# Expert tiles of the last sequence moved ahead of its attention output, and twelve instead of eight ahead of the tail

## The reference, cut to what matters

```python
def _L1_ffn_ref(x, Wg, W1, b1, W2, b2):
    logits = xt @ Wg.T
    topk_logits, topk_idx = jax.lax.top_k(logits, TOP_K)      # 2 of 8 experts for each row
    w = jax.nn.softmax(topk_logits, axis=-1)
    h = jax.nn.gelu(jnp.einsum('th,ehi->tei', xt, W1) + b1)   # 128 -> 512
    o = jnp.einsum('tei,eih->teh', h, W2) + b2                # 512 -> 128
    y = jnp.einsum('te,teh->th', gates, o)
...
x = x + linear_and_window_attention(xn) + gated_ffn(xn)
xn = _layernorm(x)
x = x + causal_attention(xn) + _L1_ffn_ref(xn)
```

## Time and profile before

| | us |
|---|---|
| median of 3 runs | 1281.19 |
| lowest, highest | 1279.73, 1285.44 |
| profiled execution | 1279.02 |
| its span, first to last instruction | 1277.3 |
| dense stage of the last sequence, from the last window score to `prefix` | 51.8 |
| maxima stage of the tail, with 29 tiles | 79.5 |
| from there to the end, with 41 tiles | 121.3 |

### The profile page before, as it was taken

One profiled execution on the slowest core, in us unless ns is written; L12 is line 12 of the kernel. 1 busy time (PEld: TensorE's weight loads), 2 busy tenths in 40 slices (PEclk: granted clock), 3 DMA queues, 4 the chain that ended last, 5 costly groups with the idle time before them and its releaser, 6 DMA issues.

```text
span 1277.3 us, 26679 instructions
## 1 busy us (share of the span) xinstructions
PE 1152.3 (90%) x9122; PEld 743.5 (58%) x9122; DVE 865.0 (68%) x3433; ACT 743.6 (58%) x1580; POOL 649.1 (51%) x846
## 2 busy tenths in 40 slices
PE   5988999998999899989998999899989867988997
PEld 2445754574457545754575457544754556874896
DVE  4066588658865886588558865886588656874563
ACT  2356357735773577457745774567546624557675
POOL 4475254535444544454444544454445435685577
PEclk9999999999999999999999999999999978999999
DMA  7601620162015301540154015401571016541233
GB/s 237 156 3 47 186 72 14 55 184 75 13 56 160 99 14 52 139 121 15 43 150 120 15 40 151 119 17 40 152 224 44 2 26 147 83 68 27 44 55 40
DMA packets 123961, 105.53 MB, mean 83 GB/s; under 512 B 15242, under 2 KB 118578, under 8 KB 123826
## 3 DMA queue, kind: packets, MB, share of 16 engines
q1 hardware_dynamic: 102162, 85.89, 24.6%
q0 software_dynamic: 13792, 9.54, 5.2%
q10 hardware_dynamic: 7872, 8.39, 1.9%
HBM read 58.59 MB, written 46.37 MB: 82 GB/s over the span
## 4 chain that ended last, share of the span: by engine, by line
PE 52%; DVE 21%; ACT 13%; issue 7%; POOL 5%; DMA 2%; DVEq 0%; SPq 0%; POOLq 0%; ACTq 0%
PE bank L701 12%; PE heads L766 12%; ACT probs L1118 8%; PE bank L680 7%; PE bank L708 7%; DVE hT_s L1586 4%; DVE xnT_s L1586 4%; DVE hrow L1586 3%; PE bank L1051 2%; PE bank L676 2%; PE bank L691 2%; PE bank L1059 2%; POOL out L1363 2%; DVE spare L1586 2%; PE bank L816 2%
## 5 line engine op out<-in xcount | busy, mean ns | idle before, releaser
L1118 ACT ACTIVATE probs<-bank 128x512 f32<-128x512 f32 (+2 forms) x896 | 442.0, 584 | 210.3 <-PE bank L708 204.5
L1310 POOL TENSOR_SCALAR_AFFINE_SELECT probs<-probs 128x384 f32<-128x384 f32 x256 | 127.2, 518 | 236.5 <-ACT probs L1118 233.6
L766 PE MATMUL heads<-probs,V 128*18 128x192 f32 (+9 forms) x3072 | 196.3, 396 | 10.6 <-POOL probs L1313 4.6
L708 PE MATMUL bank<-K,Q 128*128 128x192 bf16 (+4 forms) x1024 | 199.7, 273 | 4.6 <-DVE mx_s L1586 1.2
L708 PE MATMUL bank<-Q,K 128*128 128x192 bf16 (+4 forms) x1024 | 174.3, 274 | 16.9 <-ACT probs L1118 7.0
L1363 POOL DMA_INDIRECT out<-h1T_s x78 | 123.7, 1586 | 60.1 <-ACT h1T_s L1271 39.9
L766 PEld LDWEIGHTS heads<-probs,V 128*9 128x9 f32 (+1 forms) x3072 | 78.7, 94 | 123.3 <-issue 85.8
L708 PE MATMUL bank<-QM,K 128*128 128x512 bf16 (+3 forms) x512 | 123.8, 307 | 24.8 <-DVE mx_s L1586 17.9
L1263 ACT ACTIVATE h2T_s<-bank,h1T_s 128x128 f32<-128x128 f32 x312 | 88.9, 368 | 93.6 <-PE bank L1051 82.3
L708 PEld LDWEIGHTS bank<-Q,K 128*128 128x128 bf16 x1024 | 81.0, 98 | 88.1 <-ACT probs L1118 31.2
L708 PEld LDWEIGHTS bank<-K,Q 128*128 128x128 bf16 x1024 | 86.5, 99 | 64.5 <-DVE mx_c L1586 14.3
(11 more groups left out here) (241 smaller groups left out, 2216.8 us busy)
## 6 DMA issues: line engine op xcount, KB each, us to landing
K<-slots_of_k SPq DMA_DIRECT2D x64, 256.0 KB, 4.3
Q<-slots_of_q SPq DMA_DIRECT2D x15, 1024.0 KB, 10.1
QM<-slots_of_qm SPq DMA_DIRECT2D x8, 1024.0 KB, 9.3
h1T_s<-sorted_rows SPq DMA_DIRECT2D x78, 65.0 KB
slots_of_q<-Q SPq DMA_DIRECT2D x8, 384.0 KB, 2.6
slots_of_k<-QM SPq DMA_DIRECT2D x8, 384.0 KB, 2.9
slots_of_qm<-Q SPq DMA_DIRECT2D x8, 384.0 KB, 2.6
slots_of_k<-Q SPq DMA_DIRECT2D x8, 384.0 KB
```

The lines of the kernel that those rows point to most:

```text
L708: mm = pe.matmul(to[:, at:at + right.shape[1]], left, right, start=True, stop=True, skip_group_check=True)
L766: mm = pe.matmul(heads[ROWS * i:ROWS * i + n, P * j:P * j + widths[j]], V[:, j, g // 2, i, first:first + n], slot_of(kind, 2 * g + i // 2) ...
L1118: return act.activation(to, bank, func, scale=scale, bias=bias).then_inc(taken_sem(run, unit), 1)
L1310: pool.affine_select(out=three, in_=three, compare_op=ALU.is_ge, fill=0.0, base=0, pattern=[[0, 3], [1, P]], channel_multiplier=-1)
```

## The change

The first tiles no longer wait for `mix_first`. They begin at the head of the dense stage: PE turns and starts tile 0 ahead of `weigh(SLIDE, 2)`, finishes tile 0 behind it, tile 1 behind `weigh(SLIDE, 3)`, tile 2 behind `turn_heads`, tiles 3 and 4 behind `mix_first`, two behind the projection of `q2`, and five ahead of the tail. So twelve tiles stand ahead of the tail and 25 instead of 29 beside the maxima. DVE stages tiles 0 to 3 before it copies the heads; POOL adds tiles 0 to 2 ahead of the power; SP loads tiles 10 to 13 behind the fetch of keys and queries, ahead of the tail's wait.

```diff
-MIXED, QUERIED, ROUTED, AT_MAXIMA = 2, 3, 8, 37
+WEIGHED, TURNED, MIXED, QUERIED, ROUTED, AT_MAXIMA = 2, 3, 5, 7, 12, 37
@@ SP, body
                             fetch("k2", half, sem)
                             fetch("q2", half, sem)
+                        load_tiles(XB + 2, ROUTED + 2)
@@ SP, tail
-                loaded, pads = XB + 2, 0
+                loaded, pads = ROUTED + 2, 0
@@ PE, dense_stage
+                else:
+                    begin_tiles(run)
                 weigh(now, SLIDE, 2)
+                if not after:
+                    run_tiles(0, 1)
...
                 weigh(now, SLIDE, 3)
+                if not after:
+                    run_tiles(1, WEIGHED)
...
                 turn_heads(run, now, SLIDE, 1)
+                if not after:
+                    run_tiles(WEIGHED, TURNED)
...
-                    begin_tiles(run)
-                    run_tiles(0, MIXED)
+                    run_tiles(TURNED, MIXED)
@@ POOL, body
+                if not after:
+                    for i in range(TURNED):
+                        add_tile(i)
                 power(now, 2)
...
-                    for i in range(QUERIED):
+                    for i in range(TURNED, QUERIED):
                         add_tile(i)
@@ DVE, dense_stage
+                    if not after:
+                        for i in range(2):
+                            stage_tile(i)
+                        for i in range(2):
+                            take_xT(i)
+                        run_tiles(0, WEIGHED)
                     copy_heads(now, SLIDE, 1)
...
                     divide_rows(run, now, SLIDE, 1)
+                    if not after:
+                        run_tiles(WEIGHED, TURNED)
...
                     stats(now, 2, x1, EPS_LN)
                     if not after:
-                        for i in range(2):
-                            stage_tile(i)
-                        for i in range(2):
-                            take_xT(i)
-                        run_tiles(0, MIXED - 1)
+                        run_tiles(TURNED, MIXED - 1)
```

## The result

| | before | after |
|---|---|---|
| median of 20 runs each, us | 1280.63 | 1283.23 |
| lowest, highest | 1278.10, 1285.45 | 1279.41, 1285.59 |
| profiled execution | 1279.02 | 1284.9 |
| its span | 1277.3 | 1283.2 |

The changed kernel takes 1.002 times as long (95% interval 1.0011 to 1.0028): 2.6 us by the medians. It is a small loss. I had forecast 1279.5 us, a small gain of 0.5 us; the range, 1273 to 1287, held the time.

The account below looks back on a forecast made before the run. PE, busy 90% of the span, was taken as the bound. Terms of +6.6, -5.4 and +6.15 us up to `prefix` and -7.8 in the maxima stage netted -0.5: 1278.5 as profiled, 1280.7 by median, forecast 1279.5, range 1273 to 1287.

Parts of the forecast that it names:

- Stretch A: From the last window score to the end of `mix_first`: 6.6 us later, with three tiles done.
- Stretch B: From the end of `mix_first` to the turn of `hrow`: 7.9 us instead of 13.3, five tiles done instead of two.
- Stretch C: From the turn of `hrow` to `prefix`: 29.9 us, 6.15 longer, 3.25 of them for tile 10's load.
- The extra tile in front of the choice: Between `q2` and the turn of `xn`: logits and choice of experts come 2.9 us later.
- Maxima stage: From `prefix` to the last maxima, 25 tiles instead of 29: 7.8 us shorter, between 7.2 and 8.4.
- The slower one that named the right time: Rival: POOL or DVE paces the maxima stage, only half, 3.9 us, returns: 1283.4 us; chance 0.07.
- kept down at the head: Rival: PE stays at the lower clock through the head, 7.6 us more: 1287.1 us; chance 0.13.
- the loads did wait: Denies the faster rival, that loads don't wait and the clock holds: 1274.2 us; chance 0.22.
- can't pass the fetches: In Stretch C, loads of tiles 10 to 13 stay behind the fetches: 29.9 us; without that, 26.65.

Follow-up runs that it names:

- e2: Changed kernel with one tile instead of two behind the projection of `q2`, the other behind the logits, still twelve ahead of the tail; 1284.34 us, ratio 1.0029.
- e8: Changed kernel with the loads of tiles 8 to 10 ahead of the sends of `k2` and 11 to 16 behind the fetch; 1271.80 us, ratio 0.9944.
- e1: Changed kernel with the loads of tiles 8 to 10 ahead of the sends of `k2`; 1281.39 us, ratio 1.0005.
- e9: Changed kernel with the loads of tiles 14 to 16 behind the fetch instead of behind the wait for pad counts; 1279.90 us, ratio 0.9990.
- e4: Kernel before with twelve tiles ahead of the tail, no early start, loads of tiles 10 to 13 behind the fetch; 1285.47 us, ratio 1.0033.
- e10: Kernel before with twelve tiles ahead of the tail and the early loads of e8, without the early start; 1283.94 us, ratio 1.0023.
- e12: As e8, but with one tile behind `q2` instead of two; 1273.61 us, ratio 0.9945.

## Why the prediction was wrong, point by point

- **Stretch A came out right, in part by luck.** Turn 1 was expected 5.9 us behind the window score and came after 5.70; `mix_first` was to end after 21.3 and ended after 21.9 (the next turn, 1049.62). The full clock came later than said: the window from 1039 to 1041 has a mean of 0.88, where I had 1034.8 plus the 3.06 us of spread, 1037.9. So the first weighing took 2.5 us instead of 1.9 and the first tile step 2.7 instead of 1.9, and the wait in front of `mix_first`, 0.83 us where I had 1.7, made up for more than half of it.
- **Stretch B: right in kind, 1.6 us too dear.** `hrow` was to be turned 7.9 us behind `mix_first`; it took 6.3. The hole in front of the turn of tile 6 is there (2.22 us), but did not cost the clock: the turn of `hrow` took 0.60 us. So W-H is 28.17, not 29.2.
- **Stretch C: the step that failed.** I had 29.9 us: the turn of tile 10 after 20.7, when its load lands behind the fetches, and 9.2 from there to `prefix`. It took 32.68: the turn came after 22.4, and the rest took 10.3. The mechanism was right. Mis-sized was the landing of the load: I took the time at which the DMA engines come free from the profile before, 20.3 us into the stretch; here they are full until about 21.1 (1077.0) and still at 0.82 for a microsecond behind it. The change itself put the loads of four tiles there, 0.26 MB, which at the 250 GB/s of these windows is about 1 us by my estimate; no run tests that. And behind this longer wait the lower clock lasts longer: the tile after the first still takes 2.8 us, where it took 1.9 before.
- **Stretch C, two terms beneath.** Tile 8's load, issued behind the sends of `k2`, I had left at nothing, because before the change nobody waited for it. PE waited 5.04 us, but e2, which does that tile behind the logits, has no such wait and the stretch is as long: it was hidden by tile 10's. The extra tile in front of the choice I had put at 2.9 us. Without load waits the turn behind the choice comes 19.5 us into the stretch in e8 (18.9 in e1), against 14.55 before, so the tile costs 5.0 (4.3): its own turn waits 2.64 us for DVE, and then it runs at the lower clock, 3.6 us from 1061.84 to 1065.48, where I had reckoned with 1.9. This too was hidden behind tile 10's load after the change; it is why e8 stays at 28.45 and doesn't reach the 26.65 that I had without load waits. The loads together cost 32.68 - 28.45 = 4.2 us by e8 and 3.2 by e1, where I had 3.25.
- **Maxima stage: the second failed term.** I had -7.8, it gave -5.9. The price of the tiles was right (7.7 us for four once the clock is taken out, table above), and so was that the wait at the head would move to tile 14 (3.48 us). What I had put at nothing is a second fall of the clock. With fewer tiles, DVE has two row maxima more to work out, beside the experts' weights, between two takes (1105.11 and 1110.37 after, 1096.55 and 1100.06 before), and the hole in front of PE's next turn grows from 0.94 to 1.92 us, the last row of PE after. The clock fell behind it: 0.86, 0.50 and 0.79 in three windows of 2 us from 1109.72 make (0.14 + 0.50 + 0.21) x 2 = 1.7 us.
- **The sum.** -1.0 (B and A), +2.8 (C) and +1.9 (maxima) are +3.7, which turn my -0.5 into +3.2 up to the last maxima; the 121 us behind it gave 0.33 back.
- **The rivals.** The slower one that named the right time, 1283.4 with only half of the tiles given back, did so by luck: what returned was 5.9, not 3.9, what was missing there was clock, and most of the loss came in stretch C. The clock was not kept down at the head, and the loads did wait.
- **The Trainium skill**, "DMA: Bandwidth & Descriptors", section "Queues, rings and completion order", says that each DMA engine takes a queue's descriptors in ring order. The trace agrees as far as it goes: the tile whose load was issued at 1071.38 was turned only when the DMA share fell from 1.12 to 0.47. No run shows the order within one DMA engine, and full engines shared by all transfers would look the same. The same section says that completion is not first in, first out per issuing engine, so my "can't pass the fetches" holds for each DMA engine by itself and no further; no run here shows that either.

Two mistakes stand behind the short terms. In stretch C I took the landing of a load from the profile before, though the change itself puts more transfers into that queue and wants the rows earlier. And I counted as many falls of the clock as before, one in each stage, though the change makes new holes of two microseconds and more, and each of them can bring its own.

## What to carry to other kernels

Where work is moved earlier, move its loads with it: look up on the issuing queue what stands in front of each, when its buffer comes free, and when the rows will now be wanted. A wait can hide another: e2 took away the longest one and gained nothing. Here the same order of compute was 0.2% slower or 0.56% faster than before, by the place of six loads alone, and the place of three of them, ahead of the sends, was only open because the early start had freed their buffers. A wait that the profile shows is worth more than its length where the clock falls behind it, and less where another engine is nearly as late at the same place.

## What the runs showed of the hardware that I had not expected

The clock's fall can't be told from the length of the hole in front of it. The hole for DVE at the experts' weights is 1.92 us long after the change and 1.93 us in e8, and PE is busy 5.7 and 5.6 of the eight us up to its end. Two windows each, first after, then e8, same columns as above:

```profile
1109.00:1111.00 2.00, 0.20 (x2) 0.23 (x3) 1.49 (x6) 0.00 (x0) 1.24 (x1) 1.00 0.66 92
1111.00:1113.00 2.00, 2.00 (x12) 2.00 (x12) 1.89 (x10) 0.20 (x1) 0.47 (x1) 0.54 0.67 72
```

```profile
1099.00:1101.00 2.00, 0.45 (x2) 0.33 (x3) 1.62 (x7) 0.00 (x0) 1.49 (x1) 1.00 0.74 99
1101.00:1103.00 2.00, 2.00 (x18) 1.91 (x18) 1.65 (x10) 0.99 (x4) 0.22 (x1) 1.00 0.71 79
```

After the change PE works on at a granted clock of 0.54, in e8 at 1.00. All eight kernels with twelve tiles ahead have this hole, of 1.92 or 1.93 us. The clock fell behind it in three (after, e2, e9) and stayed at 1.00 in five (e1, e4, e8, e10, e12). In e9 the first layer behind it takes 1.78 us, in e8 1.13:

```profile
1105.72 0.30 PE L1051 MATMUL bank<-ident_s,h1T_s 128*128 128x128 f32 x1 [1.93 <-DVE h1T_s L1804]
1105.86 1.78 PE L1059 MATMUL bank<-h1T_s,w_in 128*128 128x128 f32 x8
```

In the earlier trace rows a hole of 1.93 us was also followed by the lower clock, and the one of 2.22 us in stretch B was not. What decides it stayed open. At this hole a fall costs about 1.7 us, so a forecast of this stage is uncertain by that much, and it is part of why stage lengths in single profiles do not add up exactly.
